# Two graph layers on one Trainium2 core: score banks, an early DMA transpose and other moves around row blocks 0 and 1

## The chip, the cores and the metric

The kernel runs on one core of a Trainium2 chip. The metric is the device time of one execution in microseconds; lower is better. Before the change it is 666.12 us (median of three runs, 664.54 to 666.35).

## What is computed

Inputs are x (4096 x 128, float32), a 0/1 adjacency matrix adj (4096 x 4096, float32), two scalars and a weight matrix (128 x 128).

```python
deg = clip(adj.sum(axis=1), 1.0); dis = deg ** -0.5
diffusion = (dis[:, None] * adj * dis[None, :]) @ x - x
norms = maximum(norm(x, axis=-1), 1e-8)
sim = x @ x.T / (norms[:, None] * norms[None, :])
attn = softmax(beta * sim * adj, axis=1)
x = layernorm(x + diffusion + sigmoid(alpha) * (attn @ x - x))
x = layernorm(x + relu(adj @ (x @ weights)))
```

## The kernel before

The 4096 rows are 32 row blocks of 128. The kernel is written with an instruction stream for each engine, in a fixed order, and semaphores between them; nothing is scheduled by a tool. A **start** turns x into unit rows, transposes them (`turn_rows`) and splits them into high and low half-precision parts (`turned_high`, `xnt_low`). The **attention** takes one row block after another, 2 at a time in a loop on every engine from block 2. The **tail** does the degree-normalised sums, the first layer norm, and the second layer.

For one row block r of the attention:

- SP loads four pieces of adjacency (`land_piece`, 512 KB each; `land` holds two row blocks). ScalarE casts each piece to bytes (`cast`, line 472). GpSimd packs the bytes of two blocks into words (`pack`, lines 322 to 334), and SP transposes the words by DMA (`turn_adj`).
- TensorE makes eight groups of 512 cosines (`cosines`, line 1004, three matmuls each) in PSUM. VectorE multiplies each group by the adjacency and keeps its maximum (`mask`, line 707). After the eighth, `row_max` gives the bias, and ScalarE does four exponentials of 1024 columns (`exps`, line 512), in the order 2, 3, 0, 1, or 0, 2, 3, 1 for block 0.
- The first half of the scores is transposed by TensorE (`turn_e`, line 1015) and read out as a high part on ScalarE (`e_high`, line 519) and a low part on VectorE (`e_low`, line 722). The second half is split by GpSimd (`ex_high`, line 342) and VectorE (`ex_low`, line 728) and transposed by two DMAs on SP's queue (`turn_ex(r, q, 0)` and `turn_ex(r, q, 1)`, line 253), here called the first and the second half of eTx.
- TensorE multiplies the transposed scores by x in eight pieces (`attend`, lines 1037 and 1040), in the order 0, 4, 1, 5, 2, 6, 3, 7; pieces 4 and 5 read the first half of eTx, pieces 6 and 7 the second. Block 0 goes in the order 0 to 7. VectorE adds the result to u (`attn_add`, line 735), which `minus_x` (GpSimd, line 361) has filled before, in four pieces of eight row blocks each.

The blocks overlap. In TensorE's `row(r)` each of eight steps holds cosines of block r+1 (steps 0 to 3) or r+2 (steps 4 to 7), an attention piece of r-1 or r (from step 3), and in every second step a transpose of the scores of r. A group of cosines waits until its PSUM bank has been masked:

```python
elif not start:
    pe.wait_ge(scores_done, r * H + (h - 1))
```

PSUM has eight banks. `ps_s` (two) takes the cosines, `ps_e[0]` and `ps_e[1]` the transposed scores, `ps_acc` and `ps_e[3]` the attention of even and odd blocks. `ps_e[2]` and `ps_at` are used in the start and in the tail, `ps_e[2]` by cosines of block 0 too. In the start, the unit rows are four pieces (`unit_rows`): piece 0 on VectorE (line 659), pieces 1 to 3 on GpSimd (line 304).

The names b, q and k count groups of four blocks, the buffer of two, and blocks of a group; packed_done, cast_done and the like are the semaphores.

Of the kernel before, what the change touches and what calls it, by code (L numbers as in the profile page):

```python
# [26 lines left out]
ALU = mybir.AluOpType  # L27
# [10 lines left out]
P = 128  # L38
# [14 lines left out]
def two_layer_gnn(nc, x, adj, alpha, beta, weights, out):  # L53
    N, D = x.shape
    R = N // P
    G = 4
# [17 lines left out]
    with ExitStack() as ctx:  # L74
# [153 lines left out]
        def score_bank(h, start):  # L228

            return ps_e[:, h - 2 if h < 4 else h - 4, :] if start and h % 4 >= 2 else ps_s[:, h % 2, :]  # L230

# [3 lines left out]
        def _(sp):  # L235
# [30 lines left out]
            turn_ex(0, 0, 1)  # L266
            with sp.Fori(1, Q) as b:
                for k in range(G):
                    r, q = b * G + (k - G), k % 2
                    for i in range(C):  # L270
                        sp.wait_ge(cast_done, b * (G * C) + ((k - 2) * C + i + 1))
                        land_piece(b, k, i)
                    if q == 0:
                        turn_adj(b * 2 + (k // 2 - 2), k // 2)
                    turn_ex(r + 1, 1 - q, 0)
                    turn_ex(r + 1, 1 - q, 1)
            turn_adj(R // 2 - 2, 0)
            for r in (R - 3, R - 2, R - 1):
                turn_ex(r, r % 2, 0)
                turn_ex(r, r % 2, 1)  # L280
            turn_adj(R // 2 - 1, 1)
            sp.wait_ge(e_turned, R * TB)
# [11 lines left out]
        def _(pool):  # L294
# [68 lines left out]

            unit_rows(1)
            unit_rows(2)
            unit_rows(3)
            pool.wait_ge(sign_done, 1)
# [19 lines left out]
            pool.wait_ge(sigma_done, 1)  # L387
            for q in range(C):
                minus_x(q)
            pack(2, 0, 1, 1, first=True)  # L390
            ex_high(2, 0, 0)
            ex_high(2, 0, 1)
            def two_rows(r, m, s):

                sign_block(r + 2, 0, 2 - 2 * s)
                pack(r + 1, 1, m, s)
                ex_high(r + 1, 1, 0)
                ex_high(r + 1, 1, 1)
                sign_block(r + 3, 1, 3 - 2 * s)
                pack(r + 2, 0, m + 1, 1 - s)  # L400
                ex_high(r + 2, 0, 0)
                ex_high(r + 2, 0, 1)
# [40 lines left out]
        def _(act):  # L443
# [40 lines left out]
            squares(1)  # L484
            norm_root(0)
            norm_root(1)
            squares(2)
            block_squares(3, 0)
# [15 lines left out]
            cast(0, 0, 3, first=True)  # L504
            cast(1, 1, 0, first=True)

            def exps(r, q, i, order=EXP_ORDER):
# [25 lines left out]
            exps(0, 0, 2, FIRST_EXP)  # L533
            cast(1, 1, 1, first=True)
            e_high(0, 0, first=True)
# [91 lines left out]
        def _(dve):  # L627
# [27 lines left out]

            def unit_rows(q):

                dve.wait_ge(rnorm_done, q + 1)
                nc.vector.tensor_tensor(
                    early[:, q * CH:(q + 1) * CH].rearrange("p (r d) -> p r d", d=D), x_keep[:, q * TC:(q + 1) * TC, :],  # L660
                    norm_r[:, q * TC:(q + 1) * TC].unsqueeze(2).to_broadcast([P, TC, D]),
                    ALU.mult).then_inc(xn_done[q], 1)

            def xnt_low(g):
# [3 lines left out]

            norms2(0)
            norms2(1)  # L670
            rnorm(0)
            rnorm(1)
            unit_rows(0)
            norms2(2)
            rnorm(2)
            xnt_low(0)
            norms2(3)
            xnt_low(1)
            rnorm(3)
            nc.vector.tensor_reduce(great, norm[:, :], AX.X, ALU.max).then_inc(great_done, 1)  # L680
# [140 lines left out]
            def row(r, q, second=False, spread=None):  # L821
                for h in range(H):
                    if h < C:
                        mask(r + 1, 1 - q, h + C)
                    else:
                        mask(r + 2, q, h - C)
                    if h % 2 == 0:
                        e_low(r, h // 2)
                    if h == 1:
                        ex_low(r, q, 1)  # L830
                    if h == 3:
                        row_max(r + 1, 1 - q)
                    if h == 3 and spread:
                        stage_block(spread[0], spread[0], (spread[1],))
                    if h == 5:
                        if second:
                            dve.wait_ge(u_init, C)
                        attn_add(r - 1, 1 - q)
                    if h == 7:
                        ex_low(r + 1, 1 - q, 0)  # L840
                    if h in (3, 4, 6):
                        total_step(r, q, (3, 4, 6).index(h))

            row(1, 1, second=True)
            with dve.Fori(2, R - 15, 2) as r:
                row(r, 0)
                row(r + 1, 1)
# [124 lines left out]
        def _(pe):  # L972
# [19 lines left out]
            def cosines(r, q, h, start=False):  # L992
# [5 lines left out]
                if start and h in (4, 5):  # L998
                    pe.wait_ge(scores_done, h - 3)
                elif not start:  # L1000
                    pe.wait_ge(scores_done, r * H + (h - 1))
                o = h * BANK
# [234 lines left out]
```

## Time and profile before

| | |
|---|---|
| median of three runs | 666.12 us |
| lowest, highest | 664.54, 666.35 us |
| the profiled execution | 664.73 us |
| its span, first to last instruction | 663.0 us |
| mean granted TensorE clock | 0.996 of full |
| busy: TensorE (PE), VectorE (DVE), ScalarE (ACT), GpSimd (POOL) | 639.7, 518.3, 412.6, 236.7 us |
| DMA | 107.37 MB, mean 162 GB/s |

The profile is of one execution. Its times count from the start of the span. A row of a timeline gives the start and the duration of an instruction, or of several alike in a row, in us; a bracket behind it gives the idle time of the engine before it and what ended that. A busy TensorE is not always one at its peak, as matmuls overlap and their ends are modelled. PEclk is the granted clock as a share of full speed. The attention runs from about 17 to about 434 us, the tail from there to the end.

### The profile page before, as it was taken

To read this page: it belongs to the slowest core of one execution; us is meant where nothing else is said; L and a number is where in the kernel's file an instruction comes from. 1 tells how busy PE (TensorE), PEld (TensorE's weight loads), DVE (VectorE), ACT (ScalarE), POOL (GpSimd) and SP (SyncE) were. 2 spreads that over 40 slices of the span, in tenths; PEclk is the share of its full clock that TensorE was granted. 3 is DMA by queue.
4 is the path that set the end of the run, shared out by engine and by line. 5 is a ranking of instruction groups with operands and counts; after the bars stand their busy time and mean duration, and the time that the engine had idled before them with its cause. 6 is when DMAs were issued, how large, how long until landed. Compare 5 with 4: busy or idle time off the path is not lost. (4 is left out here: it accounts for less than half of the span.)

```text
span 663.0 us, 16214 instructions
## 1 busy us (share of the span) xinstructions
PE 639.7 (96%) x5087; PEld 463.8 (70%) x5087; DVE 518.3 (78%) x1566; ACT 412.6 (62%) x768; POOL 236.7 (36%) x248
## 2 busy tenths in 40 slices
PE   7788999999999999999999999999999999999996
PEld 7455677777777777677777776788888864444465
DVE  5987789999899899899999999877777773333443
ACT  7997899999999999899999998611111110000000
POOL 4897454464463553553553557400000000000000
PEclk9998999999999999999999999999999999999999
DMA  7899999999999999999999955400000000000000
GB/s 280 297 257 232 242 277 249 252 291 237 262 285 237 278 269 238 248 286 243 287 264 236 288 128 96 86 1 1 0 0 0 0 0 1 16 17 16 16 33 33
DMA packets 165021, 107.37 MB, mean 162 GB/s; under 512 B 144385, under 2 KB 148609, under 8 KB 164993
## 3 DMA queue, kind: packets, MB, share of 16 engines
q1 hardware_dynamic: 164992, 107.04, 60.9%
q8 instruction: 12, 0.20, 0.1%
q14 instruction: 17, 0.13, 0.1%
HBM read 69.27 MB, written 2.10 MB: 108 GB/s over the span
## 5 line engine op out<-in xcount | busy, mean ns | idle before, releaser
L1004 PE MATMUL ps_s<-xn_parts,xn_signed 128*128 128x512 f16 x756 | 203.8, 380 | 4.1 <-DVE cmax L707 4.0
L707 DVE CUSTOM_DVE_ANT_1 scores<-ps_s,adj_bytes 128x512 f32<-128x512 f32 x252 | 171.4, 682 | 29.1 <-PE ps_s L1004 19.5
L512 ACT ACTIVATE scores<-scores,col 128x1024 f32<-128x1024 f32 x128 | 157.3, 1232 | 1.4 <-DVE col L718 1.1
L472 ACT ACTIVATE adj_bytes<-land 128x1024 uint8<-128x1024 f32 x128 | 133.5, 1047 | 1.3 <-POOL packed L334 1.3
L342 POOL TENSOR_SCALAR e_parts<-scores 128x1024 f16<-128x1024 f32 x64 | 69.3, 1083 | 163.2 <-ACT scores L512 151.3
L1157 PE MATMUL ps_e<-y_parts,stage 128*128 128x256 f16 x896 | 98.0, 273 | 0.0
L1004 PEld LDWEIGHTS ps_s<-xn_parts,xn_signed 128*128 128x128 f16 x756 | 68.6, 98 | 40.3 <-DVE cmax L707 3.5
L1157 PEld LDWEIGHTS ps_e<-y_parts,stage 128*128 128x128 fp8e4 x896 | 87.7, 98 | 10.1
L519 ACT ACTIVATE eT_parts<-ps_e 128x512 f16<-128x512 f32 x128 | 76.0, 595 | 29.8 <-PE ps_e L1015 28.8
L728 DVE SCALAR_TENSOR_TENSOR e_parts<-scores,e_parts 128x1024 f16<-128x1024 f32 x64 | 87.4, 1365 | 1.1 <-POOL e_parts L342 1.1
L722 DVE SCALAR_TENSOR_TENSOR eT_parts<-ps_e,eT_parts 128x512 f16<-128x512 f32 x128 | 87.5, 683 | 0.8 <-ACT eT_parts L519 0.8
L1015 PE MATMUL ps_e<-ident,scores 128*128 128x128 f32 x512 | 77.6, 275 | 1.1 <-ACT scores L512 1.1
L609 ACT ACTIVATE scores<-ps_s 128x512 f32<-128x512 f32 (+1 forms) x9 | 4.9, 550 | 108.6 <-PE ps_s L1185 108.6
L586 ACT ACTIVATE std<-mv,col 128x1 f32<-128x1 f32 x32 | 9.4, 295 | 88.3 <-DVE mv L897 88.3
L1185 PE MATMUL ps_s<-stage,x_parts 128*128 128x512 fp8e4 (+1 forms) x320 | 56.9, 336 | 0.0
L1015 PEld LDWEIGHTS ps_e<-ident,scores 128*128 128x128 f32 x512 | 54.0, 141 | 3.6 <-ACT scores L512 2.0
L1185 PE MATMUL ps_s<-land,x_parts 128*128 128x512 fp8e4 x256 | 56.4, 379 | 0.0
L1037 PE MATMUL ps_e<-x_parts,eTx 128*128 128x256 f16 x256 | 49.4, 274 | 5.1 <-DMA eTx<-e_parts 5.1
L804 DVE TENSOR_SCALAR stage<-packT 128x256 uint32<-128x256 uint32 (+1 forms) x192 | 42.5, 285 | 13.8 <-PE ps_e L1157 13.8
L1037 PE MATMUL ps_e<-x_parts,eT_parts 128*128 128x256 f16 x256 | 49.8, 275 | 1.6 <-DVE eT_parts L722 1.5
L1037 PE MATMUL ps_acc<-x_parts,eT_parts 128*128 128x256 f16 x256 | 49.2, 273 | 1.9 <-DVE eT_parts L722 1.9
L331 POOL TENSOR_TENSOR packed<-packed,adj_bytes 128x256 uint32<-128x256 uint32 x48 | 48.6, 1013 | 2.7
(129 smaller groups left out, 969.3 us busy)
## 6 DMA issues: line engine op xcount, KB each, us to landing
land<-in_adj SPq DMA_DIRECT2D x128, 512.0 KB, 5.4
x_keep<-in_x SPq DMA_DIRECT2D x4, 512.0 KB, 5.3
out<-u SPq DMA_DIRECT2D x7, 256.0 KB, 2.1
eTx<-e_parts SPq DMA_TRANSPOSE x64, 4.3
packT<-packed SPq DMA_TRANSPOSE x16, 6.6
out<-u SPq DMA_DIRECT2D x2, 128.0 KB, 1.9
scores<-in_L_gnn_weights SPq DMA_DIRECT2D x1, 64.0 KB, 3.5
col<-in_L_gnn_beta SPq DMA_DIRECT2D x1, 0.5 KB, 7.3
```

Of the source, the lines that this page charges most:

```text
L342: nc.gpsimd.tensor_scalar(e_parts[:, n, 0, :], scores[:, q, (n + 2) * CH:(n + 3) * CH], E_SCALE, 1.0, ALU.mult, ALU.mult).wait_op(sign_don ...
L472: nc.scalar.activation(adj_bytes[:, q, i * CH:(i + 1) * CH], land[:, q, i, :], ACT.Copy, scale=float(BYTE_TOP[q] >> i), accum_out=deg[:, i ...
L512: nc.scalar.activation(piece, piece, ACT.Exp, bias=neg_max[q], scale=abs_beta, accum_out=csum[:, q, i:i + 1]).then_inc(exp_done, 1)
L519: nc.scalar.activation(eT_parts[:, b, 0, :], ps_e[:, b % 2, :], ACT.Copy, scale=E_SCALE).then_inc(e_hi, 1)
L707: nc.vector.tensor_tensor_reduce(scores[:, q, o:o + BANK].rearrange("p (k q) -> p k q", k=K), score_bank(h, r == 0 if start else False).re ...
L722: nc.vector.scalar_tensor_tensor(eT_parts[:, b, 1, :], ps_e[:, b % 2, :], E_SCALE, eT_parts[:, b, 0, :], ALU.mult, ALU.subtract).then_inc( ...
L728: nc.vector.scalar_tensor_tensor(e_parts[:, n, 1, :], scores[:, q, (n + 2) * CH:(n + 3) * CH], E_SCALE, e_parts[:, n, 0, :], ALU.mult, ALU ...
L1004: ins = nc.tensor.matmul(score_bank(h, start), xn_signed[:, q, part, :], xn_parts[:, other, o:o + BANK], start=(part == 0 and other == 0), ...
L1015: ins = nc.tensor.transpose(ps_e[:, b % 2, n * P:(n + 1) * P], scores[:, q, t * P:(t + 1) * P], ident[:, :])
L1037: nc.tensor.matmul(attn_ps[q][:, 0:2 * D], hi, x_parts[:, t, :], start=(k == 0 and n == 0), stop=(k == H - 1 and n == TH - 1), skip_group_ ...
L1157: ins = nc.tensor.matmul(ps_e[:, n, 0:2 * D], stage8[n][:, b, :, k], y_tiles[t], start=(t == 0), stop=(t == R - 1))
L1185: ins = nc.tensor.matmul(ps_s[:, q, 0:rows * P], x_parts[:, t, part * D:(part + 1) * D], quads8[q if rows == G else 1][:, b, k, n:n + rows ...
```

## The change

1. **Four score banks.** From block 1 on, group h of the cosines goes to `ps_s[0]`, `ps_s[1]`, `ps_e[2]` or `ps_at`, by h modulo 4, and waits until group h-4 is masked. Block 0 keeps its banks.
2. **A transpose between loads.** The first half of eTx of row block 1 is issued between the second and the third load of row block 4. Before, it stood behind the fourth load and the adjacency transpose.
3. **A new turn of SP.** The turns of blocks 1 to 3 of the first group are written out, and an iteration now begins with the second half of a block and ends with the first half of the next.
4. **All unit rows on GpSimd.** VectorE's `unit_rows` goes; its `rnorm(0)` stands before `norms2(1)`, `rnorm(3)` before `xnt_low(1)`. ScalarE does `squares(2)` before `norm_root(1)`.
5. **The cast of piece 1 of block 1** is moved in ScalarE's order ahead of block 0's exponentials.
6. **`minus_x` in pieces.** GpSimd does one piece before the packing of block 2, one behind it, and one behind each high part of block 2. VectorE's first `attn_add` waits for one piece, and its row block 2 for all four.

```diff
         def score_bank(h, start):
-            return ps_e[:, h - 2 if h < 4 else h - 4, :] if start and h % 4 >= 2 else ps_s[:, h % 2, :]
+            if h % 4 < 2:
+                return ps_s[:, h % 2, :]
+            if start:
+                return ps_e[:, h - 2 if h < 4 else h - 4, :]
+            return ps_e[:, 2, :] if h % 4 == 2 else ps_at[:, :]
...
             turn_ex(0, 0, 1)
-            with sp.Fori(1, Q) as b:
+            for i in range(C):
+                sp.wait_ge(cast_done, 2 * C + i + 1)
+                land_piece(1, 0, i)
+                if i == 1:
+                    turn_ex(1, 1, 0)
+            turn_adj(0, 0)
+
+            def turn(b, k):
+
+                r, q = b * G + (k - G), k % 2
+                turn_ex(r, q, 1)
+                for i in range(C):
+                    sp.wait_ge(cast_done, b * (G * C) + ((k - 2) * C + i + 1))
+                    land_piece(b, k, i)
+                if q == 0:
+                    turn_adj(b * 2 + (k // 2 - 2), k // 2)
+                turn_ex(r + 1, 1 - q, 0)
+            for k in range(1, G):
+                turn(1, k)
+            with sp.Fori(2, Q) as b:
                 for k in range(G):
-                    r, q = b * G + (k - G), k % 2
-                    for i in range(C):
-                        sp.wait_ge(cast_done, b * (G * C) + ((k - 2) * C + i + 1))
-                        land_piece(b, k, i)
-                    if q == 0:
-                        turn_adj(b * 2 + (k // 2 - 2), k // 2)
-                    turn_ex(r + 1, 1 - q, 0)
-                    turn_ex(r + 1, 1 - q, 1)
-            turn_adj(R // 2 - 2, 0)
-            for r in (R - 3, R - 2, R - 1):
-                turn_ex(r, r % 2, 0)
+                    turn(b, k)
+            for r in range(R - G, R):
                 turn_ex(r, r % 2, 1)
+                if r == R - G:
+                    turn_adj(R // 2 - 2, 0)
+                if r < R - 1:
+                    turn_ex(r + 1, (r + 1) % 2, 0)
...
-            unit_rows(1)
-            unit_rows(2)
-            unit_rows(3)
+            for q in range(C):
+                unit_rows(q)
...
             pool.wait_ge(sigma_done, 1)
-            for q in range(C):
-                minus_x(q)
+            minus_x(0)
             pack(2, 0, 1, 1, first=True)
+            minus_x(1)
             ex_high(2, 0, 0)
+            minus_x(2)
             ex_high(2, 0, 1)
+            minus_x(3)
...
             norm_root(0)
+            squares(2)
             norm_root(1)
-            squares(2)
...
             cast(1, 1, 0, first=True)
+            cast(1, 1, 1, first=True)
...
             exps(0, 0, 2, FIRST_EXP)
-            cast(1, 1, 1, first=True)
             e_high(0, 0, first=True)
...
             norms2(0)
+            rnorm(0)
             norms2(1)
-            rnorm(0)
             rnorm(1)
-            unit_rows(0)
             norms2(2)
             rnorm(2)
             xnt_low(0)
             norms2(3)
+            rnorm(3)
             xnt_low(1)
-            rnorm(3)
...
                         if second:
-                            dve.wait_ge(u_init, C)
+                            dve.wait_ge(u_init, 1)
...
             row(1, 1, second=True)
+            dve.wait_ge(u_init, C)
...
                 elif not start:
-                    pe.wait_ge(scores_done, r * H + (h - 1))
+                    pe.wait_ge(scores_done, r * H + (h - 3))
```

SP's queue around row block 1, before: from the last load of row block 4 to the first half of eTx.

```order
L271 REGISTER_ALU
L241 ISA [waits cast_done]
L241 DMA land<-in_adj 128x1024
L246 ISA
L247 ISA [waits packed_done]
L247 DMA_TRANSPOSE packT<-packed 128x4x128 [waits x_loaded0]
L252 ISA
L253 DMA_TRANSPOSE eTx<-e_parts 128x16x128 [waits ex_lo,x_loaded0]
```

The same queue now, from the last load of row block 3, with the second half of block 0 behind it.

```order
L245 DMA land<-in_adj 128x1024 [waits cast_done]
L257 DMA_TRANSPOSE eTx<-e_parts 128x16x128 [waits ex_lo,x_loaded0]
L245 DMA land<-in_adj 128x1024 [waits cast_done] x2
L257 DMA_TRANSPOSE eTx<-e_parts 128x16x128 [waits ex_lo,x_loaded0]
L245 DMA land<-in_adj 128x1024 [waits cast_done] x2
L251 DMA_TRANSPOSE packT<-packed 128x4x128 [waits packed_done,x_loaded0]
L257 DMA_TRANSPOSE eTx<-e_parts 128x16x128 [waits ex_lo,x_loaded0]
```

The first half of block 1 (the second transpose of eTx in these rows) now stands ahead of two loads and of the adjacency transpose that it stood behind; the second half of block 1 is the last row.

GpSimd behind the signed rows of block 3, before: u is what `minus_x` fills, packed the words of block 2, e_parts the high parts of block 2.

```order
L361 TENSOR_SCALAR u<-x_keep,col 128x1024 [waits x_lo,sigma_done]
L361 TENSOR_SCALAR u<-x_keep,col 128x1024 [waits x_lo] x3
L322 TENSOR_TENSOR packed<-adj_bytes 128x256 [waits cast_done]
L325 TENSOR_TENSOR packed<-packed,adj_bytes 128x256 [waits pack_step]
L334 TENSOR_TENSOR packed<-packed,adj_bytes 128x256 [waits pack_step]
L342 TENSOR_SCALAR e_parts<-scores 128x1024 [waits ex_turned0,exp_done,sign_done]
L342 TENSOR_SCALAR e_parts<-scores 128x1024 [waits ex_turned1,exp_done,sign_done]
```

The same place now.

```order
L379 TENSOR_SCALAR u<-x_keep,col 128x1024 [waits x_lo,sigma_done]
L340 TENSOR_TENSOR packed<-adj_bytes 128x256 [waits cast_done]
L343 TENSOR_TENSOR packed<-packed,adj_bytes 128x256 [waits pack_step]
L352 TENSOR_TENSOR packed<-packed,adj_bytes 128x256 [waits pack_step]
L379 TENSOR_SCALAR u<-x_keep,col 128x1024 [waits x_lo]
L360 TENSOR_SCALAR e_parts<-scores 128x1024 [waits ex_turned0,exp_done,sign_done]
L379 TENSOR_SCALAR u<-x_keep,col 128x1024 [waits x_lo]
L360 TENSOR_SCALAR e_parts<-scores 128x1024 [waits ex_turned1,exp_done,sign_done]
L379 TENSOR_SCALAR u<-x_keep,col 128x1024 [waits x_lo]
```

Three of the four pieces of u have moved behind the packing and between the high parts; the last piece stands behind a high part that waits for the second half of block 1 (ex_turned1).

## Rows read from the trace of the kernel before

**Rows 1.** The page's first part: engines' busy us, share of the span, instructions.
```profile
PE 639.7 (96%) x5087; PEld 463.8 (70%) x5087; DVE 518.3 (78%) x1566; ACT 412.6 (62%) x768; POOL 236.7 (36%) x248
```

**Rows 2.** Windows: PE, PEld, DVE, ACT, POOL busy us; granted clock, DMA share, GB/s.
```profile
17.00:41.50 24.50, 19.33 (x120) 10.37 (x117) 22.12 (x58) 22.65 (x42) 22.37 (x18) 1.00 0.90 274
53.00:56.00 3.00, 3.00 (x17) 1.77 (x15) 0.87 (x3) 0.61 (x2) 2.75 (x5) 0.50 1.05 220
100.00:200.00 100.00, 100.00 (x851) 73.39 (x849) 93.21 (x239) 93.26 (x165) 49.42 (x53) 1.00 0.99 260
```

**Rows 3.** TensorE's timeline: start, us, instruction, idle before and its releaser.
```profile
23.86 1.46 PE L1004 MATMUL ps_s<-xn_parts,xn_signed 128*128 128x512 f16 x6 [1.34 <-DVE cmax L707]
...
30.27 0.82 PE L1004 MATMUL ps_s<-xn_parts,xn_signed 128*128 128x512 f16 x3 [1.69 <-DVE cmax L707]
...
41.58 0.66 PE L1015 MATMUL ps_e<-ident,scores 128*128 128x128 f32 x4 [0.18 <-ACT scores L512]
42.36 0.82 PE L1004 MATMUL ps_s<-xn_parts,xn_signed 128*128 128x512 f16 x3
...
49.05 0.81 PE L1004 MATMUL ps_s<-xn_parts,xn_signed 128*128 128x512 f16 x3 [0.39 <-DVE cmax L707]
52.59 0.28 PE L1037 MATMUL ps_e<-x_parts,eTx 128*128 128x256 f16 x1 [2.73 <-DMA eTx<-e_parts]
...
59.28 0.61 PE L1015 MATMUL ps_e<-ident,scores 128*128 128x128 f32 x4
...
62.34 0.61 PE L1015 MATMUL ps_e<-ident,scores 128*128 128x128 f32 x4
...
80.67 0.28 PE L1037 MATMUL ps_e<-x_parts,eTx 128*128 128x256 f16 x1 [1.36 <-DMA eTx<-e_parts]
```

**Rows 4.** ScalarE's timeline, 24 to 42 us: exponentials L512, casts L472.
```profile
24.81 1.24 ACT L512 ACTIVATE scores<-scores,col 128x1024 f32<-128x1024 f32 x1 [1.11 <-DVE col L718]
...
27.28 1.04 ACT L472 ACTIVATE adj_bytes<-land 128x1024 uint8<-128x1024 f32 x1
...
35.66 1.06 ACT L472 ACTIVATE adj_bytes<-land 128x1024 uint8<-128x1024 f32 x1 [0.71 <-POOL packed L334]
...
40.20 1.23 ACT L512 ACTIVATE scores<-scores,col 128x1024 f32<-128x1024 f32 x1
```

**Rows 5.** GpSimd's timeline: unit rows L304, high parts L342, minus_x L361.
```profile
8.89 2.76 POOL L304 TENSOR_TENSOR scores<-x_keep,norm_r 128x1024 f32<-128x1024 f32 x1 [7.29 <-DVE norm_r L654]
14.03 1.90 POOL L304 TENSOR_TENSOR scores<-x_keep,norm_r 128x1024 f32<-128x1024 f32 x1 [0.35 <-DVE norm_r L654]
27.53 1.76 POOL L342 TENSOR_SCALAR e_parts<-scores 128x1024 f16<-128x1024 f32 x1 [0.22 <-ACT scores L512]
30.27 1.05 POOL L342 TENSOR_SCALAR e_parts<-scores 128x1024 f16<-128x1024 f32 x1 [0.98 <-ACT scores L512]
49.02 4.39 POOL L361 TENSOR_SCALAR u<-x_keep,col 128x1024 f32<-128x1024 f32 x4
```

**Rows 6.** VectorE's timeline: its unit rows, and the low part of block 1.
```profile
8.72 1.17 DVE L659 TENSOR_TENSOR scores<-x_keep,norm_r 128x1024 f32<-128x1024 f32 x1
...
42.84 1.67 DVE L728 SCALAR_TENSOR_TENSOR e_parts<-scores,e_parts 128x1024 f16<-128x1024 f32 x1
```

**Rows 7.** SP's queue in the timeline: start and us of the issues.
```profile
40.54 4.78 SPq L241 DMA_DIRECT2D land<-in_adj  x4
...
47.44 5.37 SPq L253 DMA_TRANSPOSE eTx<-e_parts  x2
...
100.11 5.02 SPq L253 DMA_TRANSPOSE eTx<-e_parts  x2
```

**Rows 8.** eTx: issue to landing (47.4 to 50 us; whole span), and its first use in a steady row.
```profile
eTx<-e_parts SPq DMA_TRANSPOSE x1, 5.1
...
eTx<-e_parts SPq DMA_TRANSPOSE x64, 4.3
...
105.14 0.27 PE L1037 MATMUL ps_e<-x_parts,eTx 128*128 128x256 f16 x1
```

More of the change, by code:

```diff
@@ L654, in rnorm @@
                 nc.vector.reciprocal(norm_r[:, q * TC:(q + 1) * TC], norm[:, q * TC:(q + 1) * TC]).then_inc(rnorm_done, 1)
[L656 to L662, printed above, removed]
             def xnt_low(g):
```

## The prediction

> **What bounds the kernel now.** I read the counts of page and clock first, then windows by stage, then TensorE's timeline, then those of the engines that release it. TensorE (PE) is busy for 639.7 of 663.0 us [rows 1]. From 100 to 200 us it is busy for all of 100.00, at the full granted clock, with VectorE (DVE) and ScalarE (ACT) at 93 [rows 2]. So the steady rows are bound by TensorE, whose work the change leaves alone; only places where TensorE is late can pay. From 17 to 41.5 us it is busy for 19.33 of 24.50, while GpSimd (POOL) is at 22.37, ACT at 22.65, DVE at 22.12 [rows 2]: a start in which three feeding engines are full.
>
> TensorE's timeline gives the yardstick. A transpose (0.44), two cosine groups (0.65 each) and two attention pieces (0.66 each) take 3.06 us (59.28 to 62.34 [rows 3]); four of these are a row block, 12.24. An idle time in brackets is 0.16 to 0.17 less than the delay, since the modelled end of a group lies that much behind the point where the next may begin (0.61 for the transpose, 0.81 for the cosines [rows 3]). Row block 1 starts its first transpose at 41.58, row block 2 at 59.28 [rows 3]: 17.70 instead of 12.24, so 5.46 lost. It holds the wait of 2.73 for the transposed half "eTx" that ends at 52.59 [rows 3], and behind it the granted clock is 0.50, the lower of the two levels (1.2 instead of 2.4 GHz), from 53 to 56 us [rows 2]. That stretch lasts about 3.3 us and loses half of it, 1.65. It follows the longest idle time after the start; those of 1.34 and 1.69 [rows 3] had left the clock at 1.00 [rows 2].
>
> **The unit rows.** Four on POOL instead of one on DVE (1.17 us [rows 6]) and three on POOL. Those took 1.90 alone [rows 5] and 2.76 while DVE ran its own beside it [rows 5]; that neighbour goes away, so I take 1.90. The first reciprocal now stands before the second reduction, so POOL starts near 7.4 instead of 8.89 and ends at 7.4 + 4 x 1.90 = 15.0, against 14.03 + 1.90 = 15.93. The last transposes of x wait for the chain of the largest norm on DVE, not for POOL, and that chain keeps its instructions. So this edit: 0. With 2.76 each it ends at 18.4, 2.5 late; that is the upper bound, and 0.5 early the lower. The Trainium skill (GPSIMD Engine Reference, 4.1 Engine selection) speaks against the move: elementwise work with two inputs is about twice as slow there as on VectorE. That would be 4 x 2.34, an end at 16.8, and 0.9 us lost in the sum; the 1.90 beside 1.17 is a factor of 1.6, and I go by the row.
>
> **The cast in ScalarE's gap.** ACT stands idle 1.11 before its first exponential at 24.81 [rows 4]. The cast at 27.28 (1.04 [rows 4]) moves into that gap, which costs nothing as long as its adjacency piece has landed. The third exponential starts at 27.76 instead of 28.80. POOL waited 0.98 for it and is now limited by its own instruction before (27.53 + 1.76 [rows 5]), so it gains 0.95. POOL is one unbroken chain from there to the packing that releases the cast at 35.66 [rows 4]. That cast, one more and the three exponentials that begin behind them end in the one at 40.20 [rows 4], which releases 41.58. Beside it runs DVE's chain, which gains 0.53 (the low part of the first transposed scores no longer waits for ACT). TensorE gets between these two, **0.85 us**: row block 1 starts near 40.7.
>
> **Four score banks.** Block r's score group h may start once group h-4 is masked, not h-2. The waits of 1.34, 1.69 and 0.39 for cmax [rows 3] go. The first two come back: the cosines behind 23.86 run at 22.6, and the transposes behind them still need the exponential of 24.81, so TensorE then idles over 2 us in one piece; the products behind 30.27 still need DVE's low parts. I put the banks at 0 before row block 1. Inside it they free 0.34 at its first cosines (42.36 where 41.58 + 0.44 would do [rows 3]) and 0.56 at 49.05 (0.39 idle), together **0.9**. POOL's signed rows may hold back 0.5 of the latter; the half below lands later than that, so the sum is the same.
>
> **The transpose between loads, and the new turn of SP.** Before, SP's queue holds four loads, issued from 40.54 to 45.32 because the last waits for a cast [rows 7], the adjacency transpose, and only then block 1's first half at 47.44 [rows 7], which lands 5.1 us later [rows 8], 52.5. Its data are there at 42.84 + 1.67 = 44.5 [rows 6]. Now it stands behind two loads only, so it goes when DVE is done: 0.7 earlier by the start, 43.85. It lands at 48.95 to 49.1. TensorE, with the 0.85 and 0.9, wants it at 49.05 + 0.65 - 1.75 = 48.0, and waits 1.1 instead of 2.9. So **1.8** from the wait and **1.65** from the clock, if 1.1 us of idling keeps it up, as the 1.69 did. The two loads behind it are issued some 5 us later; their casts stand in row block 2, some 5 us behind their landing. In the loop the order of SP's transfers is the same; only the place of the branch moves, in front of the second half, which is needed half a row later.
>
> **The minus_x pieces.** All four of the 4.39 us at 49.02 [rows 5] ran before the packing. Now one does, one follows the packing, one each high part. DVE needs one for its first attn_add, near 51.7, and POOL has it at 49.2, so the early add is covered. All four are wanted before DVE's row block 2, near 56.1; the third high part waits for the landing of block 1's second half (near 55.5), so the fourth piece ends near 57.7. DVE stands 1.6 us. That is late next, and mostly covered: TensorE first needs DVE's output of that block near 60, DVE has it at 59.0.
>
> **The sum.** 0.85 + 0.9 + 1.8 + 1.65 = 5.2. Given back at the start of row block 2: its exponential is ready at 54.4, TensorE at 54.1 (0.4), and in block 2 its half lands some 0.2 later against TensorE than before. Net **4.6 us** by row block 3. The idle 1.36 at 80.67 [rows 3], a half that took long to land, I leave. From there TensorE is full and carries the lead to the end. In the last two blocks 0.53 of waiting for a bank goes, and the wait for DVE behind it grows by as much: 0. The profiled execution took 664.73, 1.39 under the median of 666.12. Against it the sum gives 660.1; against the median **661.5 us**.
>
> **Rivals.**
> *A. The waits come back one block later.* DVE's stop at four pieces lasts longer, because the second half, now behind a first half, two loads and the adjacency transpose, lands 1.5 us later than I think; row block 3's exponential pushes TensorE. For it: POOL and SP have no slack there. Against: SP reaches this half at about 50.3, no later than before. Price 1.5 to 2.5: about 663.5.
> *B. The half lands late and the clock falls again.* It lands after 1.8 more, as the busy queues around 40 to 80 us allow, TensorE idles 2.9 and loses 1.65 once more: 661.5 + 3.5 = 665.0. The idle time of over 2 us before 26.2 could do the same, but there three other engines set the pace. Against: the loads ahead of it are issued some 2.6 us before, where they had ended only 2.1 us before its issue in the old order too. The Trainium skill (TensorE: Matmul & The Clock Gate, Part 1) says that where the clock changes varies from run to run, since its window runs freely; by it the 1.65 is won in some executions only, and the median stands near 663.2. The one drop that I see follows the one idle time above 1.7, so I keep 1.65.
> *C. Slower: the steady rows lose their cover.* There the first half is issued at 100.11 [rows 7] and first used at 105.14 [rows 8], 5.03 later; halves land after 4.3 in the median [rows 8]. The cover is 0.7. If the new turn makes them meet the loads so that they land as late as the 5.1 of the start [rows 8], each row waits 0.1, and at 5.3 it is 0.27: over 26 rows 7 us, 668.5. It decides from 5.2 us, where 26 x 0.18 eats the 4.6. Against it: the order of the transfers in the loop is unchanged, and what triggers them still follows TensorE.
> *D. Nothing moves.* The start is bound by POOL, which has more to do in sum, at 2.76 per unit row: 2.5 late, and the banks' 0.9 is then time in which TensorE would wait for POOL: 661.5 + 2.5 + 0.9 = 664.9. Against: the neighbour that slowed POOL is gone from DVE.
>
> **How the numbers follow.** My case has 0.69, A 0.14, B 0.07, C 0.05, D 0.05. My case alone spans 659.5 (the wait at 80.67 goes too, 1.4, with a little more) to 663. The range takes in A and ends short of B: 659.2 to 664.6; the rest, with results below it, is about 2 in 10. A difference of 0.3%, 2.0 us, is what this measurement can tell. Faster by more: my case and A, 0.83. Within: B and D, 0.12. Slower: C, 0.05.
>
> **What would show it.** Row block 1's first transpose near 40.7, row block 2's near 54.5; the first cast of block 2 near 34.8; block 1's half issued near 43.9 and a wait before its use of about 1 us; no stretch at clock 0.50 behind it; DVE idle 1 to 2 us near 56 to 58; TensorE full from 85 to 400. A clock drop there, a start of block 2 later than 56.5, or more than 2 us of idle TensorE between 100 and 380 would prove it wrong.

## The result and the profile after

Over 18 runs each, taken in turn on the same chips, the kernel before took 664.47 us in the median (661.92 to 666.89) and the changed kernel 661.61 (660.25 to 663.45). The ratio is 0.996, 95% interval 0.9948 to 0.9972: faster by 1.9 to 3.5 us. The three runs of the table of times before had put the kernel before at 666.12; so the forecast time of 661.5 is met, but the forecast gain of 4.6 is 2.9 in the medians. In the two profiled executions the span went from 663.0 to 659.8.

The page of the changed kernel, its first part and the granted clock in 40 slices:

```profile
PE 640.6 (97%) x5087; PEld 464.5 (70%) x5087; DVE 518.3 (79%) x1565; ACT 412.6 (63%) x768; POOL 239.0 (36%) x249
...
PEclk9899999999999999999999999999999999999999
```

The same work as in [rows 1], in less time. The granted clock (PEclk) fell elsewhere: in the second slice, not in the fourth.

TensorE's timeline of the changed kernel (start, us, instruction, idle before):

```profile
26.90 0.33 PE L1026 MATMUL ps_e<-ident,scores 128*128 128x128 f32 x1 [2.10 <-ACT scores L532]
...
41.70 0.60 PE L1026 MATMUL ps_e<-ident,scores 128*128 128x128 f32 x4
42.14 0.81 PE L1015 MATMUL ps_s<-xn_parts,xn_signed 128*128 128x512 f16 x3
...
48.83 0.82 PE L1015 MATMUL ps_s<-xn_parts,xn_signed 128*128 128x512 f16 x3 [0.41 <-POOL xn_signed L330]
...
55.47 0.65 PE L1026 MATMUL ps_e<-ident,scores 128*128 128x128 f32 x4 [0.79 <-ACT scores L532]
...
64.47 0.28 PE L1048 MATMUL ps_acc<-x_parts,eTx 128*128 128x256 f16 x1 [1.54 <-DMA eTx<-e_parts]
...
69.74 0.43 PE L1026 MATMUL ps_e<-ident,scores 128*128 128x128 f32 x2
...
77.38 0.28 PE L1048 MATMUL ps_e<-x_parts,eTx 128*128 128x256 f16 x1 [0.23 <-DMA eTx<-e_parts]
```

Row block 1 now takes 55.47 - 41.70 = 13.77 us instead of 17.70 [rows 3]. No wait for eTx is left in it. Block 2 takes 69.74 - 55.47 = 14.27, where it took 12.66 before (its next block began at 71.94): it waits 1.54 for its own first half. Block 3 waits 0.23 instead of 1.36.

The other engines, in their timelines:

```profile
25.51 1.24 ACT L532 ACTIVATE scores<-scores,col 128x1024 f32<-128x1024 f32 x1
...
65.35 1.24 ACT L532 ACTIVATE scores<-scores,col 128x1024 f32<-128x1024 f32 x1 [2.35 <-DVE col L728]
...
7.41 1.90 POOL L322 TENSOR_TENSOR scores<-x_keep,norm_r 128x1024 f32<-128x1024 f32 x1 [5.81 <-DVE norm_r L673]
10.23 1.90 POOL L322 TENSOR_TENSOR scores<-x_keep,norm_r 128x1024 f32<-128x1024 f32 x1 [0.92 <-DVE norm_r L673]
...
54.78 1.13 POOL L379 TENSOR_SCALAR u<-x_keep,col 128x1024 f32<-128x1024 f32 x1
55.99 1.89 POOL L360 TENSOR_SCALAR e_parts<-scores 128x1024 f16<-128x1024 f32 x1
57.97 1.12 POOL L379 TENSOR_SCALAR u<-x_keep,col 128x1024 f32<-128x1024 f32 x1
...
59.65 0.69 DVE L717 CUSTOM_DVE_ANT_1 scores<-ps_s,adj_bytes 128x512 f32<-128x512 f32 x1 [2.68 <-ACT adj_bytes L491]
...
44.59 1.83 SPq L257 DMA_TRANSPOSE eTx<-e_parts  x1
...
53.02 2.00 SPq L245 DMA_DIRECT2D land<-in_adj  x4
57.05 7.99 SPq L257 DMA_TRANSPOSE eTx<-e_parts  x2
```

The unit rows take 1.90 each from 7.41 on. VectorE stands idle 2.68 before block 2; it goes on at 59.65, half a us behind the last piece of u (57.97 + 1.12 = 59.09). The profile puts this wait down to a cast, but that cast had ended by 51; what came last was u (free_minus below takes this wait away). Block 1's first half is issued at 44.59 where it was 47.44 [rows 7]. Block 2's first half is issued at 57.05, two us behind four loads.

From issue to landing, for the halves issued at 44.59 and at 57.05, and a window at the granted clock (third figure from the right):

```profile
eTx<-e_parts SPq DMA_TRANSPOSE x1, 4.3
...
eTx<-e_parts SPq DMA_TRANSPOSE x1, 7.4
...
28.00:32.00 4.00, 4.00 (x16) 1.79 (x15) 4.00 (x8) 4.00 (x8) 3.58 (x4) 0.57 0.40 164
```

### The profile page after: what moved, and what is told of

The parts are those of the page before. It is cut to its first block, busy times and chain, and to the rows that moved or that the text cites. A ratio compares the mean times of both kernels' runs of the same rounds, so it can differ in the third digit from the quotient of the medians.

```text
span 659.8 us, 16155 instructions
## 1 busy us (share of the span) xinstructions
PE 640.6 (97%) x5087; PEld 464.5 (70%) x5087; DVE 518.3 (79%) x1565; ACT 412.6 (63%) x768; POOL 239.0 (36%) x249
## 4 chain that ended last, share of the span: by engine, by line
PE 86%; DVE 4%; DMA 4%; ACT 2%; issue 2%; POOL 1%; POOLq 0%; SPq 0%; DVEq 0%; ACTq 0%
PE ps_s L1196 17%; PE ps_e L1168 15%; PE ps_s L1015 11%; PE ps_e L1048 8%; PE ps_e L1026 7%; PE ps_acc L1048 7%; PE ps_at L1015 5%; PE ps_e L1015 5%; PE ps_e L1051 4%; PE ps_acc L1051 4%; DMA eTx<-e_parts 3%; DVE scores L717 1%; DMA x_keep<-in_x 1%; PE ps_e L1064 1%; DVE e_parts L738 1%
## 5 line engine op out<-in xcount | busy, mean ns | idle before, releaser
L1015 PE MATMUL ps_s<-xn_parts,xn_signed 128*128 128x512 f16 x384 | 103.8, 381 | 0.5 <-POOL xn_signed L330 0.4
L717 DVE CUSTOM_DVE_ANT_1 scores<-ps_s,adj_bytes 128x512 f32<-128x512 f32 x128 | 87.3, 684 | 13.5 <-issue 6.7
L717 DVE CUSTOM_DVE_ANT_1 scores<-ps_e,adj_bytes 128x512 f32<-128x512 f32 x66 | 45.1, 685 | 11.3 <-PE ps_e L1015 11.2
L814 DVE TENSOR_SCALAR stage<-packT 128x256 uint32<-128x256 uint32 (+1 forms) x192 | 42.6, 287 | 13.8 <-PE ps_e L1168 13.8
L1015 PE MATMUL ps_e<-xn_parts,xn_signed 128*128 128x512 f16 x198 | 53.4, 380 | 0.0
L1015 PE MATMUL ps_at<-xn_parts,xn_signed 128*128 128x512 f16 x186 | 50.9, 383 | 0.0
```

Of the source, the lines that this page charges most:

```text
L717: nc.vector.tensor_tensor_reduce(scores[:, q, o:o + BANK].rearrange("p (k q) -> p k q", k=K), score_bank(h, r == 0 if start else False).re ...
L1015: ins = nc.tensor.matmul(score_bank(h, start), xn_signed[:, q, part, :], xn_parts[:, other, o:o + BANK], start=(part == 0 and other == 0), ...
```

## The experiments

Each kernel has a profile of one execution and 10 to 12 timed runs against the kernel before on its chip. Single executions of one program differ by 3 to 8 us, so ratios overlap much, and the readings below rest on stages of the traces, one execution each. The table gives, in us, the first exponential (E), the first transposes of row blocks 1 to 4 (S1 to S4), read from the timelines of ScalarE and TensorE, and where the clock was at 0.50 for about 3.4 us. (After TensorE's last instruction the clock is at 0.50 again in every trace; that is left out.)

The timed runs say something on the clock too, as each has its mean granted clock. One stretch of 3.41 us at 0.50 in 660 us takes the mean to 0.997 or less (3.41 x 0.5 / 660 = 0.0026). So a run at 0.998 or more had no such stretch; one at 0.997 may have had it or not. The column "no fall" counts the runs at 0.998 or more.

| kernel | E | S1 | S2 | S3 | S4 | lower clock from | no fall | ratio to before |
|---|---|---|---|---|---|---|---|---|
| before | 24.81 | 41.58 | 59.28 | 71.94 | 85.70 | 53 | 12 of 104 | 1 |
| changed | 25.51 | 41.70 | 55.47 | 69.74 | 82.42 | 28.3 | 10 of 18 | 0.996 (0.9948 to 0.9972) |
| banks_alone | 25.62 | 42.39 | 60.95 | 73.19 | 88.28 | 27.9, 51.8 (twice as long) | 0 of 12 | 1.0011 (0.9987 to 1.0035) |
| turn_alone | 25.21 | 41.98 | 55.86 | 72.08 | 84.32 | 66.7 | 2 of 12 | 0.9987 (0.9966 to 1.0008) |
| no_turn | 24.63 | 41.53 | 56.88 | 69.17 | 83.09 | 26.1 | 0 of 12 | 0.9973 (0.9957 to 0.9989) |
| rnorm3_back | 26.52 | 42.23 | 56.12 | 71.30 | 83.53 | 16.7 | 3 of 12 | 0.9966 (0.9948 to 0.9985) |
| squares_back | 27.62 | 43.33 | 57.21 | 73.68 | 86.41 | 17.1, 68.3 | 3 of 10 | 0.9965 (0.9939 to 0.999) |
| x0_2_between | 25.87 | 42.76 | 55.88 | 69.88 | 83.50 | 27.4 | 5 of 12 | 0.9947 (0.9925 to 0.9969) |
| free_minus | 24.80 | 40.98 | 54.52 | 72.02 | 84.83 | 65.8 | 2 of 12 | 0.9964 (0.9937 to 0.9991) |
| before_warm | 25.54 | 42.30 | 58.53 | 71.29 | 85.50 | nowhere | 8 of 12 | 0.9958 (0.9934 to 0.9982) |
| two_waits | 25.27 | 41.43 | 55.20 | 67.48 | 85.16 | 27.8, 79 | 2 of 12 | 0.9971 (0.9944 to 0.9999) |
| warm_start | 24.59 | 40.75 | 54.28 | 72.01 | 84.25 | 66.4 | 1 of 12 | 0.9976 (0.9951 to 1.0) |
| all_three | 26.26 | 42.45 | 56.23 | 68.50 | 80.74 | nowhere | 12 of 12 | 0.9936 (0.9916 to 0.9957) |
| cast_back | 25.85 | 42.62 | 56.49 | 70.72 | 83.09 | 28.4 | 5 of 12 | 0.9978 (0.9952 to 1.0003) |

From S4 to the end the kernel before takes 577.3 us and the changed one 577.4, so the gain between these two traces is made by S4. The others take 576.1 to 578.4; that spread is nearly as large as the gain, so a lead at S4 in one trace is not yet a gain at the end.

Of the runs of the kernel before, those at 0.998 or more have a median of 662.2 us and the others one of 664.9; in the changed kernel it is 660.8 and 662.7. By these groups (two of them of 12 and 10 runs, so an estimate) the change gains 1.4 to 2.2 us at like clock, and the rest because more of its runs are free of falls: 10 of 18 against 12 of 104. The 104 were timed beside the experiments.

**banks_alone: the kernel before with the four banks.**

```diff
-                    pe.wait_ge(scores_done, r * H + (h - 1))
+                    pe.wait_ge(scores_done, r * H + (h - 3))
```

(and `score_bank` of the change.)

> Kernel before with the four score banks alone. Theory: what the banks free before row block 1 comes back at the next wait, and inside it the landing of the first half of eTx (52.5) sets the end, so TensorE's wait there grows by what the banks free and row block 2 starts near 59.3 as before: 0 +- 0.5 us in all. Rival (the banks are what pays): row block 2 starts 0.9 or more earlier, -0.9 to -3 us.

Measured: 665.12 against 664.69, ratio 1.0011. E to S1 takes 16.77, as before (24.81 to 41.58). Inside block 1 its first cosines start 0.50 behind the transposes instead of 0.78 [rows 3], and the wait for eTx is 2.88 instead of 2.73: the little that the banks freed turned into that wait. The block even takes 18.56, since the lower clock began inside the wait and lasted twice as long. No timed run reaches 0.998. A gain of the banks alone is not shown, as the theory had it (the interval leaves room for 0.9 us).

**turn_alone: the kernel before with SP's part of the change**, both the early transpose and the new turn (the diff's first `turn_ex(1, 1, 0)` hunk and `turn`).

> Kernel before with SP's order of the change alone (first half of row block 1 between the loads, and the rotated turn). Theory: the half is issued at 44.6 instead of 47.44 and lands near 49.0 to 49.7, where TensorE wants it at 49.7; the wait of 2.73 and the stretch at clock 0.50 behind it are gone, row block 2 starts 3 to 4.5 us earlier (the unit pieces of u, all four ahead of the packing, now hold DVE), and 2 to 4 us are left at the end. Rival (banks are needed for it): under 1 us.

Measured: 663.96 against 664.69, ratio 0.9987. The wait in block 1 is gone without the banks: the block takes 13.88, 3.8 less. But S4 is only 1.4 earlier: block 2 waits 2.03 for its own first half, the clock falls behind that, and the block takes 16.22. The theory was right on block 1. At the end the median gains 0.7, and the interval takes in no gain at all. That is the rival's number, but not for its reason: block 1 did not need the banks, block 2 lost the time again.

**no_turn: the changed kernel with SP's order of before.**

```diff
-            for i in range(C):
-                sp.wait_ge(cast_done, 2 * C + i + 1)
-                land_piece(1, 0, i)
-                if i == 1:
-                    turn_ex(1, 1, 0)
...
+                    turn_ex(r + 1, 1 - q, 0)
+                    turn_ex(r + 1, 1 - q, 1)
```

> Changed kernel with SP's old order. Theory: the first half of row block 1 is issued near 47.4 and lands near 52; TensorE waits some 3 us, the clock falls to 0.50 behind it, row block 2 starts near 59: 3 to 4 us slower than the changed kernel, within 0.7 us of the kernel before. Rival (the gain is spread over the parts): 1 to 2 us slower than the changed kernel.

Measured: 662.55 against 664.69, ratio 0.9973. TensorE's timeline of it at the wait, and its clock behind it:

```profile
51.84 0.28 PE L1034 MATMUL ps_e<-x_parts,eTx 128*128 128x256 f16 x1 [2.95 <-DMA eTx<-e_parts]
...
54.00:57.00 3.00, 3.00 (x28) 2.18 (x26) 2.56 (x9) 2.53 (x4) 1.90 (x3) 1.00 1.02 309
```

The wait of 3 us is there, as forecast. The clock did not fall behind it, though it had after 2.73 in the kernel before. Block 1 takes 15.35, not 17.70, and I had counted on 17.5. The theory was half wrong: the longer idle time does not decide by itself whether the clock falls. The rival is nearer: by the ratios the kernel is some 0.9 us slower than the changed one and 1.8 faster than the one before (0.7 to 2.9). So SP's order is not what most of the gain at the end hangs on. Its one trace is not the rule for the clock either: here it fell at 26.1, and no timed run reaches 0.998.

**before_warm: the kernel before with filler in the wait.**

```diff
+                    if second and h == 4:
+                        for _ in range(8):
+                            nc.tensor.matmul(ps_at[:, 0:P], ident[:, :], ident[:, :], start=True, stop=True)
                     if h >= LAG:
                         attend(r, q, h - LAG, early=second)
```

> Kernel before with 8 small matmuls into an unused bank ahead of the attention piece that waits for the first half of row block 1 (about 2.3 us of filler inside the wait of 2.9). Theory: the granted clock stays at 1.00 behind the wait, row block 2 starts 1.65 us earlier (near 57.6), 1 to 1.7 us gained. Rival (the lower clock does not cost at the end, or the waits of DMA and DVE hide it): row block 2 starts near 59 or the gain is under 0.5 us.

```profile
53.49 0.28 PE L1037 MATMUL ps_e<-x_parts,eTx 128*128 128x256 f16 x1 [1.14 <-DMA eTx<-e_parts]
...
54.00:57.00 3.00, 3.00 (x27) 2.19 (x26) 1.46 (x5) 1.21 (x4) 2.75 (x5) 1.00 1.12 247
```

TensorE idles 1.14 instead of 2.73, the clock stays at 1.00, and block 1 takes 16.23 instead of 17.70: 1.47 for the clock (1.65 forecast; the start of this execution was 0.7 late). Ratio 0.9958, 2.8 us, more than the 1 to 1.7 forecast: eight filler matmuls give about what the whole change gives, within the intervals. In this trace there is no lower clock while TensorE has work, and 8 of 12 timed runs are at 0.998 or more, against 12 of 104 for the kernel before. So the filler seems to save more than this one stretch; how is not shown.

**rnorm3_back and squares_back: which part made the start late?** The first has `rnorm(3)` behind `xnt_low(1)` again, the second `squares(2)` behind `norm_root(1)`.

```diff
             norms2(3)
-            rnorm(3)
             xnt_low(1)
+            rnorm(3)
```

> Changed kernel with the fourth reciprocal behind the second low part again (as before). Theory: this place is what makes the start 0.7 us late (largest norm at 14.54 instead of 13.87, first exponential at 25.51 instead of 24.81); with it back the first exponential starts near 24.85 and 0.6 us are gained if that lead lasts. Rival (ScalarE's wait for the third piece of x does it): first exponential stays near 25.5.

```diff
-            squares(2)
             norm_root(1)
+            squares(2)
```

> Changed kernel with ScalarE's second root ahead of the third squares again (as before). Theory: the second reciprocal is back at 8.6, the unit rows of GpSimd end about 1 us earlier, but the chain of the largest norm is unchanged: first exponential still near 25.5, 0 us. Rival (ScalarE's wait for the third piece of x makes the start late): first exponential near 24.85, 0.6 us gained.

Measured: ratios 0.9966 and 0.9965, as the changed kernel. Their first exponentials are at 26.52 and 27.62, later than in the changed kernel, not earlier: the clock fell at 16.7 and 17.1. The maximum of the norms, which stands ahead of that, came at 15.65 and 16.86. In free_minus, whose start is the changed kernel's word for word, it comes at 15.61, against 15.62 in the kernel before. And banks_alone and before_warm, whose start is the kernel before's, have it at 16.43 and 16.35. Both my theory and its rival fall: the start differs by up to 1.3 us from execution to execution (15.44 in no_turn, 16.69 in x0_2_between, with the same instructions). What it follows is the landing of the fourth piece of x: that piece lands between 9.18 (before) and 10.88 (all_three), and the maximum comes 6.1 to 6.2 us behind it in thirteen traces and 6.4 in the kernel before, in either order of the roots.

**x0_2_between: block 2's first half behind two loads too.**

```diff
                     land_piece(b, k, i)
+                    if early and i == 1:
+                        turn_ex(r + 1, 1 - q, 0)
...
-                turn_ex(r + 1, 1 - q, 0)
+                if not early:
+                    turn_ex(r + 1, 1 - q, 0)
...
-                turn(1, k)
+                turn(1, k, early=k == 1)
```

> Changed kernel with the first half of row block 2 also issued behind two loads instead of four. Theory: that half, issued at 57.05 behind four loads of 53.0 to 55.0, took 7.4 us to land because of them, and TensorE waited 1.54 for it; behind two loads it lands in 4.5 to 6 us, TensorE's wait at 64.5 is under 0.3, 1.2 to 1.5 us gained, if VectorE (idle to 59.65 for the last piece of u) is not the next bound. Rival (VectorE's stop is the bound): under 0.5 us gained.

SP's queue, the landing of the half issued at 57.18, and ScalarE's wait:

```profile
54.11 1.05 SPq L245 DMA_DIRECT2D land<-in_adj  x2
57.18 3.33 SPq L257 DMA_TRANSPOSE eTx<-e_parts  x1
...
eTx<-e_parts SPq DMA_TRANSPOSE x1, 5.6
...
65.48 1.24 ACT L535 ACTIVATE scores<-scores,col 128x1024 f32<-128x1024 f32 x1 [2.12 <-DVE col L731]
```

It lands in 5.6 instead of 7.4, and TensorE no longer waits for it. But the block takes 14.00 (14.27 in the changed kernel): block 3's exponentials wait 2.12 for VectorE, and TensorE waits 1.54 for them. Here the rival named as VectorE's stop was right. Ratio 0.9947.

**free_minus: VectorE's wait for u moved.**

```diff
-                        if second:
-                            dve.wait_ge(u_init, 1)
+                        dve.wait_ge(u_init, 1 if second else C)
...
-            dve.wait_ge(u_init, C)
```

> Changed kernel with VectorE's wait for all four pieces of u moved from the head of row block 2 to its attn_add (a wait for a constant in each turn of the loop). Theory: VectorE starts row block 2 at about 57.0 instead of 59.65, but TensorE's wait at 64.5 for the DMA stays: 0 +- 0.4 us. Rival (VectorE's stop sets the pace): 1 to 2 us gained.

```profile
56.16 0.69 DVE L717 CUSTOM_DVE_ANT_1 scores<-ps_s,adj_bytes 128x512 f32<-128x512 f32 x1 [0.16 <-DVE e_parts L738]
...
65.32 0.28 PE L1046 MATMUL ps_acc<-x_parts,eTx 128*128 128x256 f16 x1 [3.39 <-DMA eTx<-e_parts]
...
52.94 1.99 SPq L245 DMA_DIRECT2D land<-in_adj  x4
56.08 6.29 SPq L257 DMA_TRANSPOSE eTx<-e_parts  x1
...
eTx<-e_parts SPq DMA_TRANSPOSE x1, 9.2
```

VectorE goes on at 56.16. TensorE's wait for the DMA stays and is longer, 3.39, with the lower clock behind it: the half, issued 1.2 us behind the four loads, takes 9.2 us. It was issued 1.0 earlier than in the changed kernel and landed at 65.3, not earlier than the 64.4 there. No gain, as forecast. Issued 5.9 us behind them, in the kernel before, it took 5.5.

**two_waits: both edits on block 2.**

> Changed kernel with both edits on row block 2: its first half of eTx behind two loads, and VectorE's wait for all pieces of u at its attn_add. Theory: each alone left the other as the bound (14.0 us for the block with the first edit, 17.5 with the second, for 12.24 of work); together the block takes 12.3 to 12.9 us and the end comes 1 to 1.8 us sooner than in the changed kernel. Rival (a third thing bounds the block, such as GpSimd's high parts): the block still takes over 13.7.

The block takes 12.28, so nothing else bounds it. But now block 3's first half, behind four loads and the adjacency transpose, is the late one:

```profile
78.46 0.28 PE L1049 MATMUL ps_e<-x_parts,eTx 128*128 128x256 f16 x1 [3.61 <-DMA eTx<-e_parts]
```

The clock falls behind it, block 3 takes 17.68, and the ratio is 0.9971: no faster than the changed kernel, where 1 to 1.8 us of gain were expected. The wait moved one block on.

**warm_start: filler in the start.**

```diff
+            keep_busy(3)
             pe.wait_ge(top_found, 1)
...
             cosines(1, 1, 1)
+            keep_busy(7)
             turn_e(0, 0, 0, True, FIRST_EXP)
```

> Changed kernel with filler matmuls in two idle times of TensorE in the start: three before the maximum of the norms, seven before the first transposes of row block 0. Theory: the granted clock no longer falls between 16 and 32 us; from the first exponential to row block 1's first transpose it takes 16.2 us, as in the execution that had no fall there, and the spread of the runs narrows; 0 to 0.7 us gained in the median. Rival (the fall costs 1.7 wherever it lies): 1.7 us gained.

The clock stays up in the start, and E to S1 takes 16.16. That is also what it takes where the clock fell 2.5 us or more behind E (changed kernel and two_waits, 16.19 and 16.16). Where it fell 1.5 behind E (no_turn, x0_2_between) it takes 16.90 and 16.89. So a fall there costs 0 to 0.7. The clock fell behind a wait of 3.57 in block 2 instead, only 1 of 12 timed runs is at 0.998 or more, and the ratio is 0.9976: no gain in the median.

**cast_back: the cast between the exponentials again.**

> Changed kernel with the cast of piece 1 of row block 1 back between block 0's exponentials. Theory: from the first exponential to row block 1's first transpose it takes 16.77 us instead of 16.18, so 0.6 us lost, and GpSimd's second high part waits about 1 us for its exponential. Rival (VectorE's chain sets the pace there): under 0.2 us.

```profile
31.31 1.04 POOL L360 TENSOR_SCALAR e_parts<-scores 128x1024 f16<-128x1024 f32 x1 [0.98 <-ACT scores L531]
```

E to S1 takes 16.77, as in the four kernels with the old start, and GpSimd's wait of 0.98 is back [rows 5]. With the cast in the gap it takes 16.16 to 16.19 in five traces: the cast is worth 0.6 there. The other four with it are set apart by the clock: 16.90 and 16.89 where it fell 1.5 behind E, and 15.71 in rnorm3_back and squares_back, where an earlier fall had made E itself late. At the end the difference is not clear of noise (0.9978 against 0.996, the intervals overlap).

**all_three: filler in the start, both edits on block 2, and block 3's first half behind two loads (`early=k < 3`).**

> Changed kernel with the two edits on row block 2, the same place for the first half of row block 3, and the filler in the start. Theory: row blocks 1, 2 and 3 take 13.2 to 13.8, 12.3 to 12.9 and 12.24 to 12.6 us, no stretch at the lower clock: 1.5 to 3 us faster than the changed kernel. Rival (transfers pile up later instead): block 3 or 4 over 13.5 us, under 1 us gained.

```profile
56.23 0.65 PE L1027 MATMUL ps_e<-ident,scores 128*128 128x128 f32 x4 [0.79 <-ACT scores L535]
...
68.50 0.61 PE L1027 MATMUL ps_e<-ident,scores 128*128 128x128 f32 x4
...
80.74 0.61 PE L1027 MATMUL ps_e<-ident,scores 128*128 128x128 f32 x4
```

Blocks 1, 2 and 3 take 13.78, 12.27 and 12.24. The clock falls nowhere, and all 12 timed runs are at 0.998 or more. 660.44 us against 664.40, ratio 0.9936 (0.9916 to 0.9957): faster than the kernel before by 2.9 to 5.6 us. Its ratio lies 0.0024 under the changed kernel's, 1.6 us, the low end of what was expected, though the intervals overlap; they were not timed side by side. It is the fastest of all kernels here. What is left of the moving wait is 1.19 us, for the first half of block 4.

The unit rows on GpSimd and the pieces of u were not tried alone, nor the cast without the other parts. How the gain at the end divides between the parts stays open.

## Why the prediction was right, and where it was not

- **TensorE bounds the steady rows: right.** From 100 to 200 us it is full in both kernels, from 85 to 400 us it is idle for 1.0 in each, and the lead at S4 (3.28) is the lead at the end (3.2).
- **Unit rows, 0: right in sum.** 1.90 each as forecast, from 7.41. The chain ended at 16.15, not at 15.0, because the second reciprocal had to wait for the third piece of x, which I had not priced; the maximum of the norms did not wait for it, since it comes as long behind the last piece of x, to 0.1 us, as in the three other kernels with the old start. What the prediction had cited from the Trainium skill (GPSIMD Engine Reference, 4.1 Engine selection), about twice the time of VectorE, is not what the rows show: 1.90 is 1.6 times 1.17.
- **The cast in the gap, 0.85: 0.6.** E to S1 fell from 16.77 to 16.19. GpSimd's wait did go. I had priced GpSimd's chain and VectorE's; the 0.6 is near VectorE's 0.53. Which of the two set it is not shown.
- **Banks, 0 before block 1 and 0.9 in it: 0 and 0.34.** Right that the first waits come back (one idle time of 2.10 before 26.90). In block 1 the first 0.34 came (41.70 + 0.44 = 42.14). The other 0.56 did not: the signed rows held the cosines at 48.83, 0.58 behind the end of the transposes. I had named this, but booked the 0.9 in full, since the half would land later than that. It landed earlier.
- **The transpose between loads, 1.8: larger.** Issued at 44.59 (forecast 43.85, with a start 0.7 late), it landed in 4.3, not 5.1, and the wait of 1.1 never came; the whole 2.73 went, and 0.79 for ScalarE came in its place (0.4 forecast). Block 1 took 13.77; I had 40.7 to 54.5, 13.8, because ScalarE's exponential ended it in both accounts.
- **The clock, 1.65: right in size, wrong in kind.** The stretch behind the wait went, and before_warm prices it at 1.47. But it is no debt of that one wait: in 12 of the 14 traces the clock fell at least once before 90 us, at 17, at 26 to 28, at 52 or 53, at 66 to 68 or at 79. It fell after 2.10 and not after 2.95. I took "1.69 leaves it up, 2.73 does not" for a threshold. What I had cited against my 1.65 from the Trainium skill (TensorE: Matmul & The Clock Gate, Part 1), that the place of the change varies from run to run, is what the traces agree with. Over the timed runs the mean granted clock rose from 0.9950 to 0.9972: 3.3 us and 1.8 us of lost clock, a difference of 1.5 (an estimate from these means; it counts lost clock in idle time too).
- **u in pieces, a stop of 1.6, "mostly covered": the stop was 2.68.** The last piece ended at 59.09, not at 57.7. It was not the landing of block 1's second half that held it, since that came at 55.3 as forecast: GpSimd was busy with the third piece of u until 55.91, and its high part then took 1.89, where that of 30.27 [rows 5] took 1.05. The stop was covered only as long as the DMA was later still.
- **Given back, 0.6: in block 2 1.6 where 0.2 stood.** This step failed. (The other 0.4 is the wait for ScalarE at the end of block 1.) I wrote that block 2's half "lands some 0.2 later against TensorE than before". Issued 4.3 us earlier (57.05 instead of 61.33), it took 7.4 us to land instead of 5.5, so it landed only 2.4 earlier, while block 2 began 3.8 earlier. What the change made earlier now meets the four loads that SP still issues at 53 us: in the nine traces where this half was issued before the last of its four loads had landed, it landed 1.8 to 2.7 us behind that load, however early its issue. VectorE's stop bounded the block nearly as hard: without the wait for the half it still took 14.00 (x0_2_between), without the stop 17.50, with the lower clock in it (free_minus), without both 12.28 (two_waits). So rival A had the place (one block later), the size, and one of the two causes, VectorE's stop; it did not have the DMA's, and block 1's second half was not late.
- **Block 3, left at 1.36:** it waited 0.23 in this execution and 0 to 3.6 in the others. One trace could not show that this number was chance.

The sum of the profiled executions is 0.1 later at S1, 3.9 gained in block 1, 1.6 given back in block 2, 1.1 gained in block 3: 3.3. That the forecast time was met to 0.1 us is luck: the gain was forecast 1.7 too large, and the first three runs of the kernel before lay 1.65 above its later median.

## What to carry to other kernels

When a chain is shortened, write down what the shortened transfers will meet: a transfer's landing time in the trace holds for its distance from the loads in the same queue, and an edit that issues it nearer to them gives part of the gain back. Then look for the next bound beside it: here two waits of like size held block 2, and taking either away alone gained 0.3 us or nothing there. Give each late transfer its place between loads, block after block. Where TensorE is idle for 2 us or more, as here, its clock may be at stake too; a few filler matmuls inside are a cheap trial. One trace is no proof either way, but the mean granted clock of the timed runs can be counted.

## What was unexpected of the hardware

- The same idle time does or does not lower the clock. Behind waits for eTx of 2.03, 2.34, 2.73, 3.39, 3.57 and 3.61 us it fell, and inside one of 2.88; behind 2.69, 2.71 and 2.95 it did not. Behind the idle time of 2.10 us ahead of block 0's transposes, the same in nine traces with four banks and no filler, it fell in six and stayed up in three. In rnorm3_back and squares_back it fell at 17 us; the longest idle time in the 10 us before was 1.0 us in the one and 1.85 in the other. Each stretch at 0.50 lasted about 3.4 us, once twice that.
- A transposing DMA of the same size took 4.3 us to land with two loads issued 4 us before it. With four loads 5.9 us before it took 5.5, at 3.2 us 6.8 (turn_alone), at 2.0 us 7.4, at 1.6 us 8.5 (rnorm3_back) and at 1.2 us 9.2 (free_minus).
- Executions of the same start differ by up to 1.3 us in when the loads of x let it go on: their fourth piece landed at 9.24 in no_turn and at 10.48 in x0_2_between.
